# Two attention windows in sixteen steps: projections moved to even steps, short rounding and short rest moved ahead of the long ones

## Chip, cores and metric

The kernel runs on one core of a Trainium2 chip. The metric is device time in microseconds of one execution, lower is better. The engines are TensorE (PE, with its weight loads PEld), VectorE (DVE), ScalarE (ACT), GpSimd (POOL) and SyncE (SP), which here only issues transfers.

## What is computed

One transformer layer with latent attention and a gated feed-forward network side by side, on x of shape (2, 1024, 512) in float32:

```python
xn = layernorm(x)
q = rms_norm(xn @ wq_a.T, q_norm_w) @ wq_b.T      # 32 heads of 128 + 64
kv = xn @ wkv_a.T                                 # 64 latent + 64 rotary
k_nope, v = split(rms_norm(kv_c, kv_norm_w) @ wkv_b.T)
scores = (q_nope . k_nope + rope(q_pe) . rope(k_pe)) * scale   # causal
out = softmax(scores) @ v @ wo.T
return x + out + (silu(x1) * x2) @ w3.T + b3      # x1, x2 = xn @ w12.T + b12
```

## The kernel before

Three stages follow each other: `dense` (norm, latents, feed-forward), `attention`, and `combine` (output projection). The change is in `attention` alone.

Attention works on the latent keys: each head's query is projected straight into the latent space. The 32 windows are the 16 pairs of heads, each for the two batches (window w: heads of pair w // 2, batch w % 2). A window has 8 steps (u = s % 8), four for each of its two heads. A step takes two query tiles of 128 rows: the long tile of 8, 7, 6 or 5 blocks of 128 keys, and the short one of 1, 2, 3 or 4, so that every step has nine blocks in all. There are 256 steps in one stream, and each engine runs its own loop over them, held together by semaphores.

The path of a step s:

- TensorE: `scores` (L640) of the long and then of the short tile into `score_long` (two buffers) and `score_short` (one buffer; it waits for the short exponential of step s - 1). Then `transposes(s - 1)` (L657, matmuls L664) turns the short probabilities of the step before into `flip`, which has one buffer: it waits for `ptl_ready`, that is for `low_short(s - 2)`. Then `values(s - 5)` (L667). Then, in some steps, `project(n)` (L628), one of four pieces of a window's queries (n = 4 x window + piece), and once a window the block under `absorb_at` (L725): `absorb` (L609, only in every second window, for the weights of the next pair of heads) and `output_weights` (L620). Projection, absorption and output weights all write the one PSUM bank `proj`.
- VectorE: `least` (L852), the row minimum of the long and the short scores; in every second step `outputs`; then `low_long(s - 1)` (L857) and `low_short(s - 1)` (L863), what the rounding to 16 bits left over. `weights_low` (L869) does that for new weights, once per two windows.
- ScalarE: `exp` (L735) of the long and the short scores, `high_short(s - 1)` (L749) and `high_long(s)` (L742), the rounding to 16 bits, then `take(n)` (L761) of a projection, `query_high` (L756) for rotated queries, the copies after an absorption (`weights_latent`, L768, and `wo_out`, L805) and `weights_high` (L771).
- GpSimd, per half of a window's queries: four transfers that swap the halves of the rotary part (L822), `query_low` of the half before (L829, after `query_high`), two kinds of multiplies (L840, L842) and an addition (L846).
- SP: `turn(s)` (L568), the transposing transfer of the long probabilities' two 16-bit parts, used by `values(s)` five steps on (`LAG` = 5), the loads of new weights (`load_w`, `load_wo`) and the store of outputs.

`PIECE` (L524) says which projection runs in which step of a window: {step: (windows ahead, piece)}. `HIGH` says where `query_high` runs. `PIECE_FIRST` and `HIGH_FIRST` do it for the first window. A `take` waits until `query_low` of the piece four before it is done (L795), since they share a buffer.

Of the kernel before, what the change touches and what calls it, by code (L numbers as in the profile page):

```python
# [24 lines left out]
PAIRS = NH // 2  # L25
# [423 lines left out]
def attention(nc, io, scr, res):  # L449
# [9 lines left out]
    WINS = B * PAIRS  # L459
    WIN = ST  # L460
# [5 lines left out]
    with ExitStack() as ctx:  # L466
# [54 lines left out]
            return (tile(s, kind) + 1) * P  # L521


        PIECE = {0: (1, 3), 3: (2, 0), 4: (2, 1), 7: (2, 2)}  # L524
        PIECE_FIRST = {0: (1, 2), 1: (1, 3), 4: (2, 0), 5: (2, 1), 7: (2, 2)}
        HIGH = {1: (0,), 2: (1,), 5: (2,), 6: (3,)}
        HIGH_FIRST = {3: (0, 1), 6: (2, 3)}
        absorb_at, high_weights_at = lambda s: s % WIN == (2 if s < WIN else 1), lambda s: s % WIN == (3 if s < WIN else 2)

        def piece_at(s):  # L530

# [15 lines left out]
        @block.sync  # L547
        def _(sp):
            def load_w(p):
                j = p % 2  # L550
                sp.dma_start(raw[j][:].rearrange("p h c -> p (h c)"), io["wqk"][:, p, :]).then_inc(w_in[j], 16)
                sp.dma_start(wf[j][:, :, KVL:KVL + 2 * ROPE], io["wqp"][:, p, :, :]).then_inc(w_in[j], 16)

            def load_wo(pair):
                heads = slice(2 * pair, 2 * pair + 2)
                sp.dma_start(wv[:], io["wv"][:, heads, :]).then_inc(wo_in, 16)
                sp.dma_start(wo[:], io["wo"][:, heads, :]).then_inc(wo_in, 16)

            def swap_halves(k):

                c = k % 2
                sp.wait_ge(proj_out, 2 * k + 2)
                half = ROPE // 2
                for h, base in ((0, KVL), (1, 0)):
                    for to, of in ((base, base + half), (base + half, base)):
                        sp.dma_start(rot[to:to + half, c, :], qf[of:of + half, c, h, :]).then_inc(first_in[c], 16)

            def turn(s):  # L568

                sp.wait_ge(lo_ready, s + 1)  # L570
                if s >= NPT:
                    sp.wait_ge(pv_mm, s - NPT + 1)
                n = 2 * width(s, LONG)
                sp.dma_start_transpose(prob_t[:, s % NPT, 0:n // P, :], prob_hl[:, s % NHL, 0:n]).then_inc(turn_in[s % NPT], 16)

            def store(w):
                sp.wait_ge(o_ready, BLK * (w + 1))
                sp.dma_start(scr["o"][w // 2, w % 2], o[:, w % 2].rearrange("p t c -> p (t c)")).then_inc(o_out[w % 2], 16)

            load_w(0)  # L580
            load_w(1)
            for j, (dst, src) in enumerate(((ident, "ident"), (mask, "mask"))):
                sp.dma_start(dst[:], io[src]).then_inc(o_out[j], 16)
            for dst, src in ((sinT, "sinT"), (cosT, "cosT"), (kvw2, "kvw2")):
                sp.dma_start(dst[:], io[src]).then_inc(const_in, 16)
            load_wo(0)
            for k in range(2):
                swap_halves(k)
            sp.wait_ge(wl_ready, 1)
            load_w(2)  # L590
            for s in range(STEPS):
                w, u = s // WIN, s % WIN
                turn(s)
                if u == 2 and w % 2 == 1 and w + 1 < WINS:
                    sp.wait_ge(vo_mm, w + 1)
                    load_wo((w + 1) // 2)
                p = new_pair(w)
                if u == 3 and p is not None and p + 2 < PAIRS:
                    sp.wait_ge(wl_ready, p + 1)
                    load_w(p + 2)  # L600
                if u == LAG and w >= 1:
                    store(w - 1)
            store(WINS - 1)
            for j in range(2):
                sp.wait_ge(o_out[j], 16 * (WINS // 2 + 1))

        @block.tensor
        def _(pe):
# [88 lines left out]
            for s in range(STEPS + LAG):  # L697
                w, u = s // WIN, s % WIN
                if s < STEPS:
                    if u == 0 and w >= 1:  # L700
                        pe.wait_ge(ql_ready, 4 * w)
                    if s >= 2:
                        pe.wait_ge(exp_ready[LONG], s - 1)
                    scores(s, LONG)
                    if s >= 1:
                        pe.wait_ge(exp_ready[SHORT], s)
                    scores(s, SHORT)
                if s == 1:
                    pe.wait_ge(proj_out, 6)
                if 1 <= s <= STEPS:  # L710
                    transposes(s - 1)
                t = s - LAG
                if t >= 0:
                    if t % 2 == 0 and t >= 2:
                        pe.wait_ge(o_ready, t // 2)
                    values(t)
                if s < STEPS:
                    n = piece_at(s)
                    if n is not None:
                        pe.wait_ge(proj_out, n)  # L720
                        if n % 4 == 0:
                            pe.wait_ge(wl_ready, n // 8 + 1)
                            pe.wait_ge(wo_ready, w + 1)
                        project(n)
                    if absorb_at(s):  # L725
                        pe.wait_ge(proj_out, min(4 * (w + 2), 4 * WINS))
                        if w >= WINS - 2:
                            pe.wait_ge(wo_ready, w)
                        if new_pair(w) is not None:
                            absorb(new_pair(w))  # L730
                        output_weights(w)

        @block.scalar
        def _(act):
            def exp(s, kind):  # L735
                act.wait_ge(shift_ready[kind], s + 1)
                if s >= 2:
                    act.wait_ge(lo_ready if kind == LONG else flip_mm, s - 1)
                nc.scalar.activation(prob[kind][:, s % 2, 0:width(s, kind)], score_of(s, kind), ACT.Exp,  # L739
                                     bias=shift[:, s % (2 * WIN), kind:kind + 1], scale=-1.0).then_inc(exp_ready[kind], 1)  # L740
# [8 lines left out]
            def high_short(s):  # L749
                if s >= NPS:  # L750
                    act.wait_ge(pv_mm, s - NPS + 1)
                act.wait_ge(flip_mm, s + 1)
                n = width(s, SHORT)
                nc.scalar.activation(pth[:, s % NPS, 0:n], flip[:, 0:n], ACT.Copy).then_inc(pth_ready, 1)  # L754
# [29 lines left out]
            act.wait_ge(const_in, 16 * NCONST)  # L784
            for s in range(STEPS):
                w, u = s // WIN, s % WIN
                exp(s, LONG)
                exp(s, SHORT)
                if s >= 1:
                    high_short(s - 1)  # L790
                high_long(s)
                n = piece_at(s)
                if n is not None:
                    if n >= 8:
                        act.wait_ge(ql_ready, n - 7)  # L795
                    else:
                        act.wait_ge(first_low, n - 3)
                    take(n)
                for n in high_at(s):
                    query_high(n, rot_add, n - 3)  # L800
                if absorb_at(s):
                    act.wait_ge(vo_mm, w + 1)
                    if new_pair(w) is not None:
                        weights_latent(new_pair(w))
                    nc.scalar.activation(wo_out[:, w // 2, w % 2 * H // 2:(w % 2 + 1) * H // 2], of_out, ACT.Copy,  # L805
                                         scale=kvw2[:, 0:1]).then_inc(wo_ready, 1)
                if high_weights_at(s) and new_pair(w) is not None:
                    weights_high(new_pair(w))
# [42 lines left out]
        def _(dve):  # L851
# [5 lines left out]
            def low_long(s):  # L857
                dve.wait_ge(hi_ready, s + 1)
                n = width(s, LONG)
                nc.vector.tensor_tensor(prob_hl[:, s % NHL, n:2 * n], prob[LONG][:, s % 2, 0:n], prob_hl[:, s % NHL, 0:n],  # L860
                                        ALU.subtract).then_inc(lo_ready, 1)
# [55 lines left out]
            for s in range(STEPS + LAG):  # L917
                w, u = s // WIN, s % WIN
                if s < STEPS:
                    least(s, LONG)  # L920
                    least(s, SHORT)
                t = s - LAG
                if t >= 0 and t % 2 == 1:
                    outputs(t)
                if 1 <= s <= STEPS:
                    low_long(s - 1)
                    low_short(s - 1)
                if s < STEPS and high_weights_at(s) and new_pair(w) is not None:
                    weights_low(new_pair(w))


# [218 lines left out]
```

## Time and profile before

| what | value |
|---|---|
| time, median of 3 runs | 1473.96 us (1468.43 to 1487.34) |
| time of the profiled execution | 1476.83 us |
| its span, first to last instruction | 1475.1 us |
| TensorE busy over the span | 1297.4 us (88%) |
| VectorE busy | 1066.0 us (72%) |
| ScalarE busy | 939.9 us (64%) |
| GpSimd busy | 777.7 us (53%) |
| mean granted TensorE clock | 0.974 of full speed |

The span is that of one profiled execution, the median that of separate runs; the profiled execution is 2.87 us above the median. Busy time is a union over an engine's instructions, and the ends of matmuls are modelled, so a TensorE that shows as busy is not always at its peak. For lengths of TensorE work the distance from start to start is the safer reading.

### The profile page before, as it was taken

The numbers are of one execution on the slowest core, as the hardware profiler recorded it, in microseconds if no ns is written. First come the engines' busy times: TensorE is split into PE (matmuls) and PEld (weight loads), VectorE is DVE, ScalarE is ACT, GpSimd is POOL, SyncE is SP. The second block draws the span as 40 slices with busy tenths as digits, with TensorE's granted clock in tenths as the row PEclk, the third lists the DMA queues.
The fourth block names the chain that finished last, engine by engine and source line by source line (L and its number), as shares of the span: only waits on it lengthen the run. The fifth ranks groups of instructions, "written<-read, shape, count | busy, mean of one in ns | idle before, by whom it ended". The sixth has DMA issues, their size and how long they took to land. (4 is left out here: it accounts for less than half of the span.)

```text
span 1475.1 us, 32508 instructions
## 1 busy us (share of the span) xinstructions
PE 1297.4 (88%) x12930; PEld 887.4 (60%) x12930; DVE 1066.0 (72%) x1648; ACT 939.9 (64%) x1658; POOL 777.7 (53%) x759
## 2 busy tenths in 40 slices
PE   3899995899999999999988999999999998479988
PEld 3787773566666666666656666666666666234433
DVE  3755553788888889888888888888888889522321
ACT  3644541777777787787876778787787787612110
POOL 0222020877777777777766777777777872000100
PEclk9999996999999999999999999999999999799999
DMA  4011104698989989798897989889788897899995
GB/s 162 30 57 37 50 8 143 117 169 143 169 161 168 161 149 173 142 169 173 154 158 132 165 145 180 166 148 170 142 156 154 162 166 144 192 188 239 245 219 122
DMA packets 566982, 218.48 MB, mean 148 GB/s; under 512 B 508720, under 2 KB 548272, under 8 KB 566192
## 3 DMA queue, kind: packets, MB, share of 16 engines
q1 hardware_dynamic: 556336, 191.75, 69.0%
q0 software_dynamic: 10496, 24.66, 7.2%
q8 instruction: 103, 1.69, 0.5%
q14 instruction: 47, 0.39, 0.1%
HBM read 48.57 MB, written 25.17 MB: 50 GB/s over the span
## 5 line engine op out<-in xcount | busy, mean ns | idle before, releaser
L739 ACT ACTIVATE prob_long_sb<-score_long,shift_sb 128x1024 f32<-128x1024 f32 (+3 forms) x256 | 244.9, 957 | 219.3 <-DVE shift_sb L854 219.1
L860 DVE TENSOR_TENSOR prob_hl_sb<-prob_long_sb,prob_hl_sb 128x1024 f16<-128x1024 f32 (+3 forms) x256 | 335.7, 1311 | 0.0
L854 DVE TENSOR_REDUCE shift_sb<-score_long 128x1 f32<-128x1024 f32 (+3 forms) x256 | 260.0, 1016 | 71.6 <-PE score_long L654 67.8
L829 POOL TENSOR_TENSOR ql_sb<-qf_sb,qh_sb 128x512 f16<-128x512 f32 x124 | 145.0, 1170 | 204.2 <-ACT qh_sb L759 204.1
L747 ACT ACTIVATE prob_hl_sb<-prob_long_sb 128x1024 f16<-128x1024 f32 (+3 forms) x256 | 233.0, 910 | 0.0
L846 POOL TENSOR_TENSOR qf_sb<-qf_sb,rot_sb 64x512 f32<-64x512 f32 x124 | 183.7, 1482 | 9.5
L651 PE MATMUL score_long<-key_hi,qh_sb 128*128 128x512 f16 (+3 forms) x512 | 175.9, 344 | 9.5 <-DVE ql_sb L914 8.6
L685 PE MATMUL acc<-ch,prob_t_sb 128*128 128x65 f16 x1664 | 178.0, 193 | 0.0
L683 PE MATMUL acc<-ch,prob_t_sb 128*128 128x65 f16 x1664 | 177.6, 194 | 0.3 <-DMA prob_t_sb<-prob_hl_sb 0.3
L684 PE MATMUL acc<-cl,prob_t_sb 128*128 128x64 f16 x1664 | 177.7, 191 | 0.0
L664 PE MATMUL flip<-ident_sb,prob_short_sb 128*128 128x128 f32 x640 | 117.0, 281 | 65.4 <-DVE ptl_short_sb L866 65.3
L652 PE MATMUL score_long<-key_lo,qh_sb 128*128 128x512 f16 (+3 forms) x512 | 174.1, 340 | 0.0
L822 POOL DMA_DIRECT2D rot_sb<-qf_sb x248 | 124.3, 507 | 88.3 <-DVE ql_sb L914 62.1
L653 PE MATMUL score_long<-key_hi,ql_sb 128*128 128x512 f16 (+3 forms) x512 | 170.8, 340 | 0.0
L842 POOL TENSOR_TENSOR qf_sb<-qf_sb,cosT_sb 128x512 f32<-128x512 f32 x124 | 166.7, 1364 | 0.0
L685 PEld LDWEIGHTS acc<-ch,prob_t_sb 128*128 128x128 f16 x1664 | 153.3, 97 | 0.0
L684 PEld LDWEIGHTS acc<-cl,prob_t_sb 128*128 128x128 f16 x1664 | 152.9, 99 | 0.0
L683 PEld LDWEIGHTS acc<-ch,prob_t_sb 128*128 128x128 f16 x1664 | 152.4, 97 | 0.4 <-DMA prob_t_sb<-prob_hl_sb 0.4
L866 DVE TENSOR_TENSOR ptl_short_sb<-flip,pth_short_sb 128x128 f16<-128x128 f32 (+3 forms) x256 | 124.3, 485 | 22.6 <-ACT pth_short_sb L754 13.8
L739 ACT ACTIVATE prob_short_sb<-score_short,shift_sb 128x128 f32<-128x128 f32 (+3 forms) x256 | 134.2, 524 | 0.0
L664 PEld LDWEIGHTS flip<-ident_sb,prob_short_sb 128*128 128x128 f32 x640 | 68.6, 141 | 102.6 <-issue 96.7
L854 DVE TENSOR_REDUCE shift_sb<-score_short 128x1 f32<-128x128 f32 (+3 forms) x256 | 122.4, 478 | 0.2 <-PE score_short L654 0.2
(180 smaller groups left out, 3315.3 us busy)
## 6 DMA issues: line engine op xcount, KB each, us to landing
o<-o_sb SPq DMA_DIRECT2D x32, 512.0 KB, 4.1
o_nat_sb<-o SPq DMA_DIRECT2D x32, 512.0 KB, 6.7
rot_sb<-qf_sb POOLq DMA_DIRECT2D x248, 64.0 KB, 2.8
wo_sb<-wo SPq DMA_DIRECT2D x16, 512.0 KB, 4.2
wqk_sb<-wqk SPq DMA_DIRECT2D x16, 320.0 KB, 4.5
x_sb<-x SPq DMA_DIRECT2D x4, 1024.0 KB, 4.7
y<-y_sb SPq DMA_DIRECT2D x16, 256.0 KB, 2.0
prob_t_sb<-prob_hl_sb SPq DMA_TRANSPOSE x256, 4.7
```

What stands on the lines that cost most here:

```text
L651: nc.tensor.matmul(out, qh[:, row, q], key_hi[:, head, at], start=True, stop=False)
L652: nc.tensor.matmul(out, qh[:, row, q], key_lo[:, head, at], start=False, stop=False)
L653: nc.tensor.matmul(out, ql[:, row, q], key_hi[:, head, at], start=False, stop=not last)
L664: mm = nc.tensor.transpose(flip[:, at], prob[SHORT][:, s % 2, at], ident[:])
L683: nc.tensor.matmul(acc[:, at:at + KVL + 1], hi, high, start=(j == 0), stop=False)
L684: nc.tensor.matmul(acc[:, at:at + KVL], hi, low, start=False, stop=False)
L685: mm = nc.tensor.matmul(acc[:, at:at + KVL + 1], lo, high, start=False, stop=(j == i))
L739: nc.scalar.activation(prob[kind][:, s % 2, 0:width(s, kind)], score_of(s, kind), ACT.Exp, bias=shift[:, s % (2 * WIN), kind:kind + 1], sc ...
L747: nc.scalar.activation(prob_hl[:, s % NHL, 0:n], prob[LONG][:, s % 2, 0:n], ACT.Copy).then_inc(hi_ready, 1)
L846: nc.gpsimd.tensor_tensor(qf[rows, c, h, :], qf[rows, c, h, :], rot[rows, c, :], ALU.add).then_inc(rot_add, 1)
L854: nc.vector.tensor_reduce(shift[:, s % (2 * WIN), kind:kind + 1], score_of(s, kind), AX.X, ALU.min).then_inc(shift_ready[kind], 1)
L860: nc.vector.tensor_tensor(prob_hl[:, s % NHL, n:2 * n], prob[LONG][:, s % 2, 0:n], prob_hl[:, s % NHL, 0:n], ALU.subtract).then_inc(lo_rea ...
```

## The change

The projections of a window move from steps 0, 3, 4, 7 to 0, 2, 4, 6. The block under `absorb_at` moves from step 1 to step 3 and `weights_high` from step 2 to step 5 (all windows but the first), with the waits and loads that belong to them. On ScalarE `high_short(s - 1)` goes ahead of both exponentials, on VectorE `low_short(s - 1)` ahead of `low_long(s - 1)`, and `weights_low` runs one step after the `weights_high` it belongs to. No instruction of an engine is added or taken away.

```diff
-        PIECE = {0: (1, 3), 3: (2, 0), 4: (2, 1), 7: (2, 2)}
+        PIECE = {0: (1, 3), 2: (2, 0), 4: (2, 1), 6: (2, 2)}
...
-        absorb_at, high_weights_at = lambda s: s % WIN == (2 if s < WIN else 1), lambda s: s % WIN == (3 if s < WIN else 2)
+        absorb_at, high_weights_at = lambda s: s % WIN == (2 if s < WIN else 3), lambda s: s % WIN == (3 if s < WIN else 5)
...
-                if u == 2 and w % 2 == 1 and w + 1 < WINS:
+                if u == 4 and w % 2 == 1 and w + 1 < WINS:
                     sp.wait_ge(vo_mm, w + 1)
                     load_wo((w + 1) // 2)
                 p = new_pair(w)
-                if u == 3 and p is not None and p + 2 < PAIRS:
+                if u == (7 if w else 3) and p is not None and p + 2 < PAIRS:
                     sp.wait_ge(wl_ready, p + 1)
                     load_w(p + 2)
...
                         if n % 4 == 0:
                             pe.wait_ge(wl_ready, n // 8 + 1)
+                        if n % 4 == (0 if w == 0 else 1):
                             pe.wait_ge(wo_ready, w + 1)
                         project(n)
                     if absorb_at(s):
-                        pe.wait_ge(proj_out, min(4 * (w + 2), 4 * WINS))
+                        pe.wait_ge(proj_out, min(4 * (w + 2) + (1 if w else 0), 4 * WINS))
...
+                if s >= 1:
+                    high_short(s - 1)
                 exp(s, LONG)
                 exp(s, SHORT)
-                if s >= 1:
-                    high_short(s - 1)
                 high_long(s)
...
                 if 1 <= s <= STEPS:
+                    low_short(s - 1)
                     low_long(s - 1)
-                    low_short(s - 1)
-                if s < STEPS and high_weights_at(s) and new_pair(w) is not None:
+                if s < STEPS and s > 0 and high_weights_at(s - 1) and new_pair(w) is not None:
                     weights_low(new_pair(w))
```

## Rows read from the trace of the kernel before

**Rows 1.** Stretches: start:end, length, busy us (instructions) by engine, granted clock, DMA share, GB/s.
```profile
500.00:700.00 200.00, 185.10 (x2270) 129.53 (x2271) 174.99 (x260) 155.86 (x268) 148.85 (x141) 1.00 0.91 165
```

**Rows 2.** Line 805's own answer, 600 to 700 us: duration, first and last start.
```profile
L805 ACT ACTIVATE wo_out<-proj,kvw_sb x3: 481/493/494, 611.3 to 673.9; 128x256 f32<-128x256 f32 x3
```

**Rows 3.** Waits of the whole run: who waited for whom, us, times, longest.
```profile
ACT prob_long_sb L739 <- DVE shift_sb L854: 219.1, 206, 4.3
POOL ql_sb L829 <- ACT qh_sb L759: 204.1, 119, 4.2
...
PE flip L664 <- DVE ptl_short_sb L866: 65.3, 127, 2.6
...
PE score_short L651 <- ACT prob_short_sb L739: 13.0, 62, 0.7
```

**Rows 4.** Timeline of TensorE: start us, us, line, what, idle time before it.
```profile
601.23 0.39 PE L651 MATMUL score_long<-key_hi,qh_sb 128*128 128x512 f16 x1
...
602.82 0.61 PE L664 MATMUL flip<-ident_sb,prob_short_sb 128*128 128x128 f32 x4
603.26 0.19 PE L683 MATMUL acc<-ch,pth_short_sb 128*128 128x65 f16 x1
...
604.07 0.47 PE L637 MATMUL proj<-lat_hi,wq_h_sb 128*128 128x512 f32 x1
...
605.33 0.39 PE L651 MATMUL score_long<-key_hi,qh_sb 128*128 128x512 f16 x1
...
608.31 1.08 PE L616 MATMUL proj<-wqk_sb 128*128 128x64 f32 x8
609.32 0.65 PE L624 MATMUL proj<-wo_sb,wv_sb 128*64 128x256 f32 x4
...
620.61 0.63 PE L664 MATMUL flip<-ident_sb,prob_short_sb 128*128 128x128 f32 x4 [1.20 <-DVE ptl_short_sb L866]
```

**Rows 5.** Timeline of VectorE.
```profile
615.59 1.23 DVE L871 TENSOR_TENSOR wq_l_sb<-wq_f_sb,wq_h_sb 128x512 fp32r<-128x512 f32 x1 [0.88 <-ACT wq_h_sb L773]
...
618.08 1.92 DVE L860 TENSOR_TENSOR prob_hl_sb<-prob_long_sb,prob_hl_sb 128x768 f16<-128x768 f32 x1
619.92 0.55 DVE L866 TENSOR_TENSOR ptl_short_sb<-flip,pth_short_sb 128x384 f16<-128x384 f32 x1
...
625.03 1.07 DVE L854 TENSOR_REDUCE shift_sb<-score_long 128x1 f32<-128x896 f32 x1
```

**Rows 6.** Timeline of GpSimd.
```profile
617.92 3.21 POOL L842 TENSOR_TENSOR qf_sb<-qf_sb,cosT_sb 128x512 f32<-128x512 f32 x2
```

**Rows 7.** Groups by line and shape, 340 to 1280 us: count, busy us, mean ns, idle before.
```profile
L846 POOL TENSOR_TENSOR qf_sb<-qf_sb,rot_sb 64x512 f32<-64x512 f32 x114 | 168.2, 1476 | 8.8
...
L842 POOL TENSOR_TENSOR qf_sb<-qf_sb,cosT_sb 128x512 f32<-128x512 f32 x112 | 150.5, 1363 | 0.0
...
L829 POOL TENSOR_TENSOR ql_sb<-qf_sb,qh_sb 128x512 f16<-128x512 f32 x114 | 132.3, 1161 | 188.9 <-ACT qh_sb L759 188.9
...
L822 POOL DMA_DIRECT2D rot_sb<-qf_sb x224 | 112.2, 506 | 24.8 <-ACT qf_sb L764 20.1 <-issue 4.4
...
L840 POOL TENSOR_TENSOR rot_sb<-rot_sb,sinT_sb 128x512 f32<-128x512 f32 x56 | 105.3, 1880 | 5.0 <-DMA rot_sb<-qf_sb 4.9
...
L860 DVE TENSOR_TENSOR prob_hl_sb<-prob_long_sb,prob_hl_sb 128x640 f16<-128x640 f32 x60 | 88.7, 1479 | 0.0
...
L860 DVE TENSOR_TENSOR prob_hl_sb<-prob_long_sb,prob_hl_sb 128x1024 f16<-128x1024 f32 x59 | 71.9, 1218 | 0.0
```

**Rows 8.** Timeline of ScalarE.
```profile
627.04 0.47 ACT L739 ACTIVATE prob_short_sb<-score_short,shift_sb 128x256 f32<-128x256 f32 x1
...
628.40 0.64 ACT L759 ACTIVATE qh_sb<-qf_sb 128x512 f16<-128x512 f32 x1
```

**Rows 9.** The page's costliest groups: the long values, idle time before them and its cause.
```profile
L683 PE MATMUL acc<-ch,prob_t_sb 128*128 128x65 f16 x1664 | 177.6, 194 | 0.3 <-DMA prob_t_sb<-prob_hl_sb 0.3
```

**Rows 10.** DMA issues of the page: count, KB each, median us to landing.
```profile
wo_sb<-wo SPq DMA_DIRECT2D x16, 512.0 KB, 4.2
```

## The prediction

> **What bounds the kernel now.** I began with the stretches, to see which engine is nearest to full in the stage that the change touches. In a stretch of 200 us of the attention stage [rows 1] TensorE is busy 185.10 us (92.5%) at a granted clock of 1.00, VectorE 174.99 (87%), ScalarE 155.86, GpSimd 148.85. So TensorE leads, VectorE is close behind, and even a perfect order has only some 8% to give.
>
> Next the length of the repeating unit. The copy of L805 runs once per window; from its first to its third start [rows 2] two windows took 673.9 - 611.3 = 62.6 us. Two windows are the unit, since one absorption serves both. I call this a pair; 15 of them (windows 1 to 30) make up nearly the whole stage.
>
> Then the timeline of TensorE, for what a pair must cost if nothing waits [rows 4]. Starts are used, not durations, since matmuls overlap: scores of a step 602.82 - 601.23 = 1.59; four flips 603.26 - 602.82 = 0.44, so 0.11 a block; values 604.07 - 603.26 = 0.81; a projection 605.33 - 604.07 = 1.26; an absorption 609.32 - 608.31 = 1.01; output weights some 0.6. A pair has 16 steps, 40 flipped blocks, 8 projections, one absorption and two output weights: 16 x 2.40 + 40 x 0.11 + 8 x 1.26 + 1.0 + 1.2 = 55.1 us. So 62.6 - 55.1 = 7.5 us of a pair are stalls, with their restarts.
>
> The waits say which [rows 3]: 65.3 us of TensorE before the flips of L664, for ptl_short (L866), in 127 of 256 steps, and 13.0 before the short scores, for prob_short. The reader sees the first happen at 620.61: 1.20 us idle [rows 4], ended by the low_short that VectorE ran from 619.92 to 620.47 [rows 5]. In front of that low_short stood a low_long of 1.92 us. That is the pattern that the change goes at.
>
> **The change part by part.**
>
> *low_short ahead of low_long.* The next flip waits for low_short alone, so each ptl_short comes earlier by one low_long: 1.218 us in the mean for 1024 wide, 1.479 for 640 wide [rows 7]. That is as much as the longest stall I saw on it (1.20 us). low_long comes later by one low_short (0.55 us [rows 5], less for narrower ones). Behind it are the transposing DMA and the long values, four steps on; those waited 0.3 us in the whole run [rows 9], so this costs nothing. Were that cover gone, 0.55 us a step would be 9 us a pair.
>
> *high_short ahead of both exponentials.* Without this, low_short would still wait for ScalarE to finish two exponentials. ScalarE stands idle 219.1 us before the long exponential, waiting for its minimum [rows 3], about 0.9 us a step; a high_short copies at most 512 columns, no more than a query_high, which takes 0.64 [rows 8]. It now waits for the flips of its step, and the exponentials, high_long, the takes and the roundings of queries are queued behind it. In step 5 the flip ends 0.38 + 0.11 after the long scores and one block is rounded, while the minimum takes 1.07 [rows 5]: the minimum still comes last. In steps 3 and 7 (four short blocks 0.7, three flips 0.33, up to 0.64 for the rounding, a minimum of five blocks, well under 1.07) the rounding comes last, by some 0.8 us. Behind them stand step 3's absorption or output weights and the eight long blocks (1.36) of steps 4 and 0, which come before the next short scores. So I take nothing; the bounds are 0 and 0.8 us for each of four steps a pair.
>
> *Projections in steps 0, 2, 4, 6; absorption in step 3.* No matmul is added or removed. Before, steps 3 and 4, and 7 and 0, carried 1.26 us extra each while 5 and 6 carried none. Now every light step stands beside a heavy one.
>
> What is late next is the short score. Take step 5, which has no projection before or after the change. From the start of its minimum (625.03 [rows 5]) to the end of its short exponential (627.04 + 0.47 = 627.51 [rows 8]) is 2.48 us; 0.2 us lie ahead of it after the long scores, 0.06 behind (estimates from the same timelines). So 2.74 us pass between the long scores of step 5 and the short scores of step 6. TensorE meanwhile has two short blocks (0.38), one flip (0.11), values (0.81) and six long blocks (1.04): 2.34. That leaves a stall of 0.4, with a restart of 0.1 (620.47 to 620.61 is 0.14) 0.5 us. Steps 1 to 2 do the same now that the absorption has left step 1. Four per pair: 2.0 us.
>
> *weights_low one step behind weights_high.* Now VectorE waits 0.88 us for wh and then works 1.23 us [rows 5] just ahead of step 3's minimum, once per pair. After, weights_high runs at step 5 and weights_low at the end of step 6, without the wait. The 1.23 us stay, and I let 0.9 us of them (between 0 and 1.23) reach the next short score, since step 7 is light.
>
> *The waits moved on TensorE.* wo_ready now stands ahead of the projection of step 4, the wait on proj_out ahead of the absorption of step 3. Behind each are all later matmuls. The take of step 2 ends about 1.5 us before the absorption wants it, the copy of L805 about as long before step 4's projection, by laying the row durations end to end. Nothing, unless ScalarE is late (rival 3).
>
> *The loads on SP.* load_wo goes past two more turns, load_w past four; their waits are then long met. The loads land in 4.2 us [rows 10] beside the turns, which have the slack of [rows 9]. Nothing.
>
> *GpSimd.* GpSimd and VectorE get in each other's way: low_long is slower narrow than wide [rows 7], and two multiplies of L842, 1.363 us each by the mean, took 3.21 us together [rows 6] while the 1.92 us low_long ran [rows 5]. Because take(2,0) and take(2,2) now come ahead of the second query_high, the rotation starts 0.6 us later in the step, and shorter windows push it later still, onto low_longs of steps 1 and 5 that were clean. Each hit costs VectorE the rest of one GpSimd operation, between 0 and 1.4 us; the heavy step that follows absorbs most of it. I take 0.9 us a pair, between nothing and 4 x 1.4, nearer to nothing because of that room. On this the Trainium skill, "GPSIMD Engine Reference", section "Key points", says that GpSimd contends with VectorE instructions that have two SBUF inputs; that is low_long, and not low_short, whose first input is in PSUM. By that rule alone, with every low_long of steps 1 and 5 hit, the sum would be rival 2's; by the row means unchanged, it would be 0.9 us a pair lower than mine.
>
> **Sum.** 55.1 + 2.0 + 0.9 + 0.9 = 58.9 us a pair, 3.7 less than now. Times 15: 55.5. From the profiled execution's 1476.8: 1421 us. (That execution is 2.9 us above the median of the runs, 1473.96.)
>
> **Rivals.**
>
> 1. *The reorder reaches TensorE's floor.* If short scores hardly wait, a pair is 55.1 + 0.9 + 0.9 = 56.9: 5.7 x 15 = 86, so 1391. For it: VectorE's 54.8 (174.99/200 of a pair) is below the floor. Against: the chain of 2.74 us is there already.
>
> 2. *Contention eats half.* Four low_longs per pair meet half a GpSimd operation each, 4 x 0.73 = 2.9 us, and all of it reaches the minimum and so the short score. That is 2.0 more than my 0.9, a pair of 60.9: 1.7 x 15 = 25, so 1451. For it: [rows 6, 7]. Against: steps 2 and 6 have a projection, 1.26 us, behind the short score.
>
> 3. *Slower: a loop through GpSimd.* Before, the second query_high did not stand behind a take that waits for query_low of the first. Now take(2,0) in step 2 and take(2,2) in step 6 do. That closes a loop per half window: query_low 1.16, L840 1.88, L842 2 x 1.36, L846 2 x 1.48, four issues 4 x 0.51, query_low 1.16 [rows 7], a take and a query_high at some 0.64 each [rows 8]: 13.2 us. It decides from 15.65, half a window of now, that is when low_longs hold up GpSimd by 2.5 us more per half. With 16.2 a pair is 64.9: 2.3 x 15 = 35 more, 1511. For it: low_longs slide onto the chain. Against: query_low waits 204.1 us for ScalarE [rows 3], so the chain has room today.
>
> 4. *No gain.* Each stall on ptl_short turns into one on the short score (13.0 us now [rows 3]), because VectorE's minimum is what is late in both. A pair is 62.2, 1471. For it: VectorE runs without a gap through 618.08 to 620.47. Against: half of that was low_long, which no flip waits for any more.
>
> **How the numbers follow.** Chances: forecast 0.58 (pairs of 57.6 to 59.9: 1402 to 1436), rival 1 0.08, rival 2 0.17, rival 3 0.08, rival 4 0.09. Two per cent, about what a measurement of this kernel can tell from no change, is 29.5 us, some 2.0 us a pair. The forecast, rival 1 and the better third of rival 2 (0.06) are faster: 0.72. The rest of rival 2 and rival 4: 0.20 within. Rival 3: 0.08 slower. The range from 1388 to 1455 holds the forecast, rival 1 and most of rival 2, some 0.82.
>
> **What would show it.** Right: the wait of L664 on ptl_short falls from 65.3 to under 15 us; the short score's wait rises to 25 to 50; the copy of L805 repeats every 58 to 60 us per pair; TensorE is busy over 95%; VectorE's wait for wq_h is gone. Wrong: takes that wait for ql (rival 3), low_long means at 1.7 us and over (rival 2), or waits of L651 on prob_short beyond 70 us (rival 4). The forecast falls above all if ScalarE, now tied to the flips at the head of each step, starts its long exponential later than the minimum allows.

## The result, and the profile after

The changed kernel takes 1427.97 us (median of 3 runs, 1426.66 to 1437.23) against 1473.96 us before: a ratio of 0.9677 with a 95% interval of 0.9577 to 0.9776, faster by 3.2%. The profiled execution took 1437.23 us with a span of 1435.5 us, 40 us less than before's 1475.1. All of it lies in the attention stage. From the first scores of step 0 to those of step 255 it takes 951.2 us instead of 997.6 us; what lies ahead and behind, untouched by the change, went from 477.5 to 484.2 us, and is between 469.6 and 484.2 us in the profiled executions of this document. The profiled execution of the changed kernel is also the slowest of its three runs.

The stretch that answers to [rows 1], with the same columns:

```profile
500.00:700.00 200.00, 190.98 (x2373) 137.15 (x2373) 174.86 (x274) 167.27 (x285) 154.40 (x147) 0.99 0.98 174
```

TensorE went from 185.10 to 190.98 us of 200, 3.2% more, at a granted clock of 0.99 instead of 1.00, and 2373 matmuls stand in that time instead of 2270, 4.5% more. (The stretch begins at another place of a pair in the two traces, so the two shares can't be set against each other closely.) The transfer engines' share is 0.98, not 0.91. The two stretches behind it are less full:

```profile
700.00:900.00 200.00, 187.96 (x2351) 135.04 (x2348) 177.40 (x274) 166.47 (x282) 158.42 (x150) 1.00 0.93 168
900.00:1100.00 200.00, 189.99 (x2368) 136.55 (x2367) 177.55 (x272) 166.12 (x285) 153.46 (x147) 0.99 0.92 163
```

The copy that runs once per window, as in [rows 2], but from its first to its 31st start:

```profile
L806 ACT ACTIVATE wo_out<-proj,kvw_sb x31: 469/483/487, 308.5 to 1198.9; 128x256 f32<-128x256 f32 x31
```

That is (1198.9 - 308.5) / 15 = 59.4 us a pair, where 62.6 stood and 58.9 was forecast. Taken from the first scores of window 1 to those of window 31, as in all that follows, a pair was 62.72 before and is 59.47 now. The gain of 3.25 times 15 is 49 us; the first window gives 3.4 of it back (37.3 us instead of 33.9).

The waits of the changed kernel, those that answer to [rows 3] and the new ones (who waited for whom: us, times, longest):

```profile
POOL ql_sb L830 <- ACT qh_sb L760: 149.7, 79, 4.3
...
ACT pth_short_sb L755 <- PE flip L664: 115.7, 157, 3.0
...
POOL rot_sb L841 <- DMA rot_sb<-qf_sb: 39.7, 22, 3.9
...
ACT prob_long_sb L740 <- DVE shift_sb L855: 31.2, 80, 1.1
...
PE score_long L651 <- POOL ql_sb L830: 26.5, 27, 2.7
PE score_short L651 <- ACT prob_short_sb L740: 24.8, 67, 1.1
...
ACT qf_sb L765 <- POOL ql_sb L830: 9.4, 6, 1.6
...
DVE wq_l_sb L872 <- ACT wq_h_sb L774: 0.4, 1, 0.4
```

The line's own answer for the flips lists all that ended TensorE's idle time before them, and it is one line:

```profile
  ACT prob_short_sb L740: 2.6, 2
```

So the 65.3 us before the flips are gone. ScalarE's 219.1 us before the long exponential became 31.2, and 115.7 us now stand one instruction earlier, before high_short. The short scores wait 24.8 us instead of 13.0. And there is a wait that the prediction did not have: 26.5 us before the first long scores of a window, for GpSimd's query_low. GpSimd itself has less room: its wait for query_high fell from 204.1 to 149.7 us, and 39.7 us now go to waiting for the rotary swaps.

### The profile page after: what moved, and what is told of

It is laid out like the page before. It is cut to its first block and busy times, and to the rows that moved or that the text cites. A ratio compares the mean times of both kernels' runs of the same rounds, so it can differ in the third digit from the quotient of the medians.

```text
span 1435.5 us, 32537 instructions
## 1 busy us (share of the span) xinstructions
PE 1280.1 (89%) x12930; PEld 891.0 (62%) x12930; DVE 1033.0 (72%) x1648; ACT 950.3 (66%) x1658; POOL 772.0 (54%) x759
## 5 line engine op out<-in xcount | busy, mean ns | idle before, releaser
L861 DVE TENSOR_TENSOR prob_hl_sb<-prob_long_sb,prob_hl_sb 128x1024 f16<-128x1024 f32 (+3 forms) x256 | 319.3, 1247 | 0.0
L740 ACT ACTIVATE prob_long_sb<-score_long,shift_sb 128x1024 f32<-128x1024 f32 (+3 forms) x256 | 244.6, 955 | 31.4 <-DVE shift_sb L855 31.2
L830 POOL TENSOR_TENSOR ql_sb<-qf_sb,qh_sb 128x512 f16<-128x512 f32 x124 | 145.6, 1175 | 150.4 <-ACT qh_sb L760 149.7
L651 PE MATMUL score_long<-key_hi,qh_sb 128*128 128x512 f16 (+3 forms) x512 | 177.5, 347 | 36.1 <-POOL ql_sb L830 26.5
L847 POOL TENSOR_TENSOR qf_sb<-qf_sb,rot_sb 64x512 f32<-64x512 f32 x124 | 188.8, 1522 | 9.5
L755 ACT ACTIVATE pth_short_sb<-flip 128x128 f16<-128x128 f32 (+3 forms) x256 | 111.7, 436 | 116.6 <-PE flip L664 115.7
L843 POOL TENSOR_TENSOR qf_sb<-qf_sb,cosT_sb 128x512 f32<-128x512 f32 x124 | 172.8, 1414 | 0.0
L651 PEld LDWEIGHTS score_long<-key_hi,qh_sb 128*128 128x128 f16 x512 | 50.0, 98 | 116.7 <-issue 33.6
```

The lines of the kernel that those rows point to most:

```text
L651: nc.tensor.matmul(out, qh[:, row, q], key_hi[:, head, at], start=True, stop=False)
L843: op = nc.gpsimd.tensor_tensor(qf[:, c, h, :], qf[:, c, h, :], cosT[:, h, at], ALU.mult)
L847: nc.gpsimd.tensor_tensor(qf[rows, c, h, :], qf[rows, c, h, :], rot[rows, c, :], ALU.add).then_inc(rot_add, 1)
```

## The experiments

Ten kernels. Each ratio is to the kernel before, run beside it. A pair is from the trace as above: 15th part of the time from the first scores of window 1 to those of window 31. Before 62.72, changed kernel 59.47. Each pair is from one trace. The edit in the first window alone touches no other window, and yet its trace has 58.94: differences of half a microsecond between two traces say little.

| kernel | median us | ratio, 95% interval | pair us |
|---|---|---|---|
| both reorders, old places | 1415.98 | 0.9623 (0.9553 to 0.9693) | 59.05 |
| new places, old orders | 1437.33 | 0.9746 (0.9686 to 0.9805) | 59.68 |
| changed, ScalarE's order back | 1589.13 | 1.0789 (1.0727 to 1.0851) | 69.33 |
| changed, VectorE's order back | 1433.81 | 0.9709 (0.9653 to 0.9765) | 59.42 |
| before, ScalarE's reorder alone | 1469.87 | 0.9978 (0.9950 to 1.0006) | 62.30 |
| changed, load_w after the swaps | 1416.80 | 0.9602 (0.9561 to 0.9644) | 58.24 |
| changed, query_high ahead of take | 1406.15 | 0.9511 (0.9459 to 0.9562) | 58.49 |
| changed, weights_low at once in window 0 | 1419.12 | 0.9629 (0.9579 to 0.9679) | 58.94 |
| the last three together | 1397.33 | 0.9468 (0.9425 to 0.9512) | 57.43 |
| those, absorption back in step 1 | 1386.11 | 0.9431 (0.9375 to 0.9486) | 56.91 |

### Both reorders, old places

Edit, on the kernel before:

```diff
+                if s >= 1:
+                    high_short(s - 1)
                 exp(s, LONG)
                 exp(s, SHORT)
-                if s >= 1:
-                    high_short(s - 1)
                 high_long(s)
...
-                    low_long(s - 1)
                     low_short(s - 1)
+                    low_long(s - 1)
```

> The kernel before with the two reorders alone (short rounding first on ScalarE, short rest first on VectorE); projections, absorption and loads where they were. Theory (the reorders take away the stalls before the flips, the new places balance the steps): the wait of the flips on ptl_short falls from 65.3 to under 20 us, the time to 1440 to 1455. Rival (the places do nearly all, the reorders only change which wait ends last): 1465 to 1480, with the short score's wait on prob_short up from 13 to over 40 us.

Measured: 1415.98 us, 24 us below what the theory gave. The reorders alone do as much as the whole change or more; the intervals overlap. Idle time before the flips, from that line's answer, and two waits:

```profile
  ACT prob_short_sb L739: 2.6, 2
  issue: 0.3, 1
```

```profile
PE score_short L651 <- ACT prob_short_sb L739: 41.9, 96, 2.1
...
PE score_long L651 <- POOL ql_sb L829: 0.8, 2, 0.5
```

The flips no longer wait for ptl_short, as the theory said. What the rival said of the next wait holds too: the short scores' wait rose to 41.9 us. The time is far from the rival's.

### New places, old orders

Edit, on the changed kernel: both orders as before.

> The changed kernel with both orders put back; only the new steps of projections, absorption, weight rounding and loads are left. Theory: flips still wait for ptl_short, over 40 us, and the time is 1445 to 1465. Rival (places do nearly all): 1425 to 1435.

Measured: 1437.33 us, 2.3 us above the rival's range and below the theory's. Its interval against the kernel before, 0.9686 to 0.9805, is clear of no change, but not of a change of two per cent. From its waits:

```profile
PE score_long L651 <- POOL ql_sb L830: 21.5, 31, 2.4
...
PE score_short L651 <- ACT prob_short_sb L740: 11.0, 58, 0.2
...
PE flip L664 <- DVE ptl_short_sb L867: 8.3, 13, 1.8
```

The flips' wait fell to 8.3 us with both orders as before. That is a miss of mine: I expected over 40. The new places alone take most of those stalls away; they are projections, absorption, weight rounding and loads together, and which of these does it was not separated. So before the flips the two halves of the change do the same job. In time they do not add up either: from 62.72 us a pair, the orders alone reach 59.05, the places alone 59.68, both together 59.47. The waits show one reason. The places bring TensorE a wait on query_low, 21.5 us here and 26.5 in the changed kernel, that the old places don't have (0.8 us). Beside the reorders they lower the short score's wait, from 41.9 to 24.8 us. What the places give is hidden by what they cost: once three repairs below have taken that wait down to 3.6 us, a pair is 57.43, 1.62 below the orders alone. The repairs were not run on the old places, so how much of this belongs to the places is not shown.

### Changed kernel, ScalarE's order back

```diff
-                if s >= 1:
-                    high_short(s - 1)
                 exp(s, LONG)
                 exp(s, SHORT)
+                if s >= 1:
+                    high_short(s - 1)
                 high_long(s)
```

> The changed kernel with ScalarE's order put back (both exponentials ahead of the short rounding), VectorE's short rest still first. Theory: the short rest now waits for ScalarE, with low_long queued behind it, so VectorE idles and the time rises by 10 to 30 us over the changed kernel (1438 to 1458). Rival (the rounding at the head only delays exponentials): 1420 to 1430.

Measured: 1589.13 us, over 150 us slower than the changed kernel, five times the top of what I gave it. Its waits, then a step on VectorE and on ScalarE:

```profile
ACT prob_long_sb L740 <- DVE shift_sb L855: 321.9, 254, 2.8
...
DVE ptl_short_sb L867 <- ACT pth_short_sb L755: 278.8, 255, 1.8
```

```profile
705.74 0.82 DVE L855 TENSOR_REDUCE shift_sb<-score_long 128x1 f32<-128x640 f32 x1
...
708.37 0.56 DVE L867 TENSOR_TENSOR ptl_short_sb<-flip,pth_short_sb 128x384 f16<-128x384 f32 x1 [1.22 <-ACT pth_short_sb L755]
708.85 1.75 DVE L861 TENSOR_TENSOR prob_hl_sb<-prob_long_sb,prob_hl_sb 128x768 f16<-128x768 f32 x1
710.52 1.21 DVE L855 TENSOR_REDUCE shift_sb<-score_long 128x1 f32<-128x1024 f32 x1
```

```profile
706.59 0.79 ACT L740 ACTIVATE prob_long_sb<-score_long,shift_sb 128x640 f32<-128x640 f32 x1 [0.49 <-DVE shift_sb L855]
707.28 0.68 ACT L740 ACTIVATE prob_short_sb<-score_short,shift_sb 128x512 f32<-128x512 f32 x1
707.85 0.49 ACT L755 ACTIVATE pth_short_sb<-flip 128x384 f16<-128x384 f32 x1
```

Read across the two: minimum (705.74), long exponential (706.59), short exponential (707.28), rounding (707.85), then VectorE's short rest (708.37), its long rest (708.85) and the next minimum (710.52). Each of these waits for the one before it, on two engines by turns: 255 of 256 short rests wait for ScalarE. A step is that whole circle, 4.78 us here, 69.33 / 16 = 4.33 in the mean. With low_long in front of low_short, as before, VectorE has work for the time that ScalarE takes (in the changed kernel a low_long takes 1.1 to 1.6 us in the mean, by its width); with high_short in front of the exponentials, ScalarE has it done. In the new places, only the reorder on VectorE without that on ScalarE closes the circle.

### Changed kernel, VectorE's order back

```diff
-                    low_short(s - 1)
                     low_long(s - 1)
+                    low_short(s - 1)
```

> The changed kernel with VectorE's order put back (long rest ahead of short rest), ScalarE's short rounding still first. Theory: flips wait again behind low_long, over 25 us, 1435 to 1450. Rival (with balanced steps the flips do not wait for it any more): within 5 us of the changed kernel, 1423 to 1433.

Measured: 1433.81 us, and 59.42 us a pair against 59.47. The time lies between the two ranges, 0.8 us above the rival's; the pair and the flips' wait of 7.1 us, where the theory had over 25, are the rival's. In the new places, beside ScalarE's reorder, no worth of VectorE's order can be told. Its flips:

```profile
PE flip L664 <- DVE ptl_short_sb L867: 7.1, 15, 1.3
```

### Kernel before, ScalarE's reorder alone

Formed after these four: perhaps ScalarE's order alone does it. Edit: the first half of the first diff.

> The kernel before with ScalarE's short rounding moved ahead of the exponentials and nothing else; VectorE's order and all places as before. Theory formed after the first four runs (what ends the stalls before the flips is ScalarE's order: the short rounding fills ScalarE's idle time, so that rounding and rest of the long tile follow earlier; VectorE's order adds little): 1415 to 1430, flips' wait on ptl_short under 25 us. Rival (both reorders are needed in the old places, since low_short still stands behind low_long): 1445 to 1465, flips' wait over 35 us.

Measured: 1469.87 us, a ratio of 0.9978 (0.9950 to 1.0006): no difference that can be told. My second theory fell, and the rival's flips are what the trace has, though its time is not:

```profile
PE flip L664 <- DVE ptl_short_sb L866: 50.8, 122, 1.3
```

In the old places the flips do wait for a low_short that stands behind low_long, and VectorE's reorder on top of ScalarE's is worth 62.30 - 59.05 = 3.25 us a pair. So what VectorE's reorder is worth depends on ScalarE's and on the places: a gain of 3.25 us a pair in the old places beside ScalarE's, nothing in the new places beside it (59.42 to 59.47), and a loss of 9.65 in the new places without it (59.68 to 69.33). VectorE's reorder alone in the old places was not run.

### Changed kernel, load_w after the swaps

In the changed kernel, among windows 1 to 29, the even ones take 28.2 to 31.2 us and the odd ones, which have the absorption, 28.6 to 31.8. A long even one (window 6, 443.67 to 474.88), on SP, GpSimd and TensorE:

```profile
450.90 0.57 SPq L551 DMA_DIRECT2D wqk_sb<-wqk  x1
451.52 0.43 SPq L552 DMA_DIRECT2D wq_f_sb<-wqp  x1
```

```profile
451.14 2.01 POOL L823 DMA_DIRECT2D rot_sb<-qf_sb  x4
...
461.39 1.29 POOL L841 TENSOR_TENSOR rot_sb<-rot_sb,sinT_sb 128x512 f32<-128x512 f32 x1 [3.86 <-DMA rot_sb<-qf_sb]
```

```profile
474.88 0.39 PE L651 MATMUL score_long<-key_hi,qh_sb 128*128 128x512 f16 x1 [2.65 <-POOL ql_sb L830]
```

load_w was moved to step 7, but it stands behind that step's turn, and so goes out at 450.90, 7.2 us into the next window, at the moment when GpSimd issues its swaps (451.14). The last swap lands 8.2 us after the last issue; GpSimd idles 3.86 us, and 13.5 us later the next window's first scores wait 2.65 us for query_low. Window 26 (1042.59 to 1071.25), which has no load, for comparison:

```profile
1050.06 2.01 POOL L823 DMA_DIRECT2D rot_sb<-qf_sb  x4
...
1056.41 1.27 POOL L841 TENSOR_TENSOR rot_sb<-rot_sb,sinT_sb 128x512 f32<-128x512 f32 x1
```

Its swaps land 4.2 us after the last issue, and GpSimd goes on without idling. Not every load does this. Of the twelve even windows with one, six (4, 6, 8, 16, 20, 22) take 30.1 to 31.2 us, their swaps land 6.8 to 8.2 us after the last issue, and the waits on query_low at their ends, 1.95 to 2.66 us each, make up 14.2 of the 26.5 us. In the other six the load goes out earlier, 6.4 to 6.7 us into the window (6.7 to 7.5 in the long ones), the swaps land within 6.3 us, and the window takes 28.2 to 29.1.

The longest windows have no load. They are 5, 9 and 23, each right behind such a wait, with 31.8 us where the odd windows next to them take 29.7 to 29.9. Window 5, its head, and its first scores:

```profile
411.90:443.70 31.80, 30.18 (x357) 21.78 (x358) 26.86 (x42) 24.99 (x44) 22.97 (x23) 0.95 0.73 139
412.60:415.95 3.35, 3.35 (x28) 2.46 (x27) 1.43 (x3) 0.77 (x3) 3.35 (x3) 0.50 0.95 242
```

```profile
411.85 0.39 PE L651 MATMUL score_long<-key_hi,qh_sb 128*128 128x512 f16 x1 [2.32 <-POOL ql_sb L830]
```

TensorE had waited 2.32 us for query_low (1.95 and 2.32 ahead of windows 9 and 23) and had just begun again when its granted clock fell to 0.50, the lower of its two levels, 1.2 GHz. Behind the three other waits, of 2.65, 2.33 and 2.66 us ahead of windows 7, 17 and 21, it stayed at 1.00. (The trace of the kernel before has one such fall, in window 16, behind a wait of 2.59 us before the flips.) So a wait on query_low cost its own time and, three times, some 2.1 us more: 6.3 us in all, 0.42 of a pair. Edit:

```diff
-                if u == (7 if w else 3) and p is not None and p + 2 < PAIRS:
-                    sp.wait_ge(wl_ready, p + 1)
-                    load_w(p + 2)
+                if w % 2 == 0 and u == (2 if w else 3):
+                    p = new_pair(w - 1) if w else 1
+                    if p is not None and p + 2 < PAIRS:
+                        sp.wait_ge(wl_ready, p + 1)
+                        load_w(p + 2)
```

> The changed kernel with load_w moved three turns further, to step 2 of the window after, so that it is issued after the rotary swaps of step 1 have landed. Theory (the load that the change moved to step 7 is issued late, among the swaps of the next window's step 1; these land 5 to 8 us after their issue instead of 4, GpSimd starts its rotation late and the next window's first scores wait for its query_low): the swaps of step 1 land within 4.5 us in all windows, TensorE's wait on ql falls from 26.5 to about 12 us, time 10 to 20 us below the changed kernel (1408 to 1418). Rival (GpSimd's chain is simply full, the swaps' landing is a symptom): within 5 us of the changed kernel.

Measured: 1416.80 us and a pair of 58.24, 1.23 less than the changed kernel. In this trace the clock does not fall in windows 1 to 30, which is 0.42 of the 1.23. The ratio's interval, 0.9561 to 0.9644, overlaps the changed kernel's, 0.9577 to 0.9776, so the gain in time rests on the waits in the traces:

```profile
POOL rot_sb L843 <- DMA rot_sb<-qf_sb: 19.9, 16, 2.1
PE score_long L653 <- POOL ql_sb L832: 13.0, 22, 0.9
```

The waits are as the theory had them: TensorE's on query_low fell from 26.5 to 13.0 us, the longest from 2.7 to 0.9, and GpSimd's on the swaps from 39.7 to 19.9. The landing was not always within 4.5 us: the swaps of step 1 still took 5.2 to 6.4 us in ten windows of thirty, so the load was about half of the delay, not all.

### Changed kernel, query_high ahead of take

```diff
+                if s >= WIN:
+                    for n in high_at(s):
+                        query_high(n, rot_add, n - 3)
                 n = piece_at(s)
...
-                for n in high_at(s):
-                    query_high(n, rot_add, n - 3)
+                if s < WIN:
+                    for n in high_at(s):
+                        query_high(n, rot_add, n - 3)
```

> The changed kernel with ScalarE's query_high ahead of the take of the same step (all windows but the first). Theory (the earlier take stands in front of the second query_high, GpSimd's last query_low comes 0.6 us and more later, and the next window's first scores wait for it by 0.13 to 0.65 us even in windows without a late load): TensorE's wait on ql falls from 26.5 to about 8 us, time 10 to 15 us below the changed kernel. Rival (that wait only comes from late swaps): within 5 us of the changed kernel.

Measured: 1406.15 us, a pair of 58.49.

```profile
PE score_long L651 <- POOL ql_sb L834: 11.1, 23, 1.4
```

The theory's direction holds: 26.5 us became 11.1 (8 were expected), with load_w where the changed kernel has it, and although GpSimd waits longer for the swaps (67.7 us, where the changed kernel has 39.7). The pair's 0.98 times 15 is 14.7 us, in the range given; 0.42 of the 0.98 is the clock, which does not fall in windows 1 to 30 of this trace either. The median fell by more, 21.8 us, of which the trace does not account for 7.

### Changed kernel, weights_low at once in the first window

The projection of step 4 in window 0, and what VectorE did just before:

```profile
278.37 0.77 PE L637 MATMUL proj<-lat_hi,wq_h_sb 128*128 128x512 f32 x1 [5.05 <-issue]
```

```profile
276.53 1.75 DVE L872 TENSOR_TENSOR wq_l_sb<-wq_f_sb,wq_h_sb 128x512 fp32r<-128x512 f32 x1
```

The wait is put down to "issue", but weights_low ends at 278.28, and the projection, which waits for wl_ready, starts at 278.37.

```diff
-                if s < STEPS and s > 0 and high_weights_at(s - 1) and new_pair(w) is not None:
+                if (s < WIN and high_weights_at(s) or s >= WIN and s < STEPS and high_weights_at(s - 1)) and new_pair(w) is not None:
```

> The changed kernel with weights_low in the same step as weights_high in the first window only, as before. Theory (in the first window the projection of step 4 waits for it; 5.05 us idle there against 1.66 before): the first window falls from 37.3 to about 34 us, the time by 3 us. Rival: the stall comes from elsewhere, and nothing changes.

Measured: the first window takes 33.8 us instead of 37.3, as expected. The median, 1419.12 us, is 8.9 below the changed kernel's; the 3.5 us of the window are shown, the rest is within what these medians vary by.

### The three together

> The changed kernel with all three: load_w at step 2 of the window after, query_high ahead of take, weights_low at once in the first window. Theory: the gains add up but for an overlap in the wait on ql, 20 to 30 us below the changed kernel (1398 to 1408), pairs of windows near 57.5 us. Rival (short scores and GpSimd's contention set the pace): 1412 to 1425.

Measured: 1397.33 us, at the lower end of the theory, and a pair of 57.43. The interval, 0.9425 to 0.9512, lies wholly below the changed kernel's. The wait on query_low is nearly gone; that of the short scores remains:

```profile
PE score_long L653 <- POOL ql_sb L836: 3.6, 16, 0.5
...
PE score_short L653 <- ACT prob_short_sb L742: 24.1, 67, 1.3
```

### Those, with the absorption back in step 1

```diff
-        absorb_at, high_weights_at = lambda s: s % WIN == (2 if s < WIN else 3), lambda s: s % WIN == (3 if s < WIN else 5)
+        absorb_at, high_weights_at = lambda s: s % WIN == (2 if s < WIN else 1), lambda s: s % WIN == (3 if s < WIN else 5)
...
-                        if n % 4 == (0 if w == 0 else 1):
+                        if n % 4 == 0:
                             pe.wait_ge(wo_ready, w + 1)
...
-                        pe.wait_ge(proj_out, min(4 * (w + 2) + (1 if w else 0), 4 * WINS))
+                        pe.wait_ge(proj_out, min(4 * (w + 2), 4 * WINS))
```

> The version with the three repairs, its absorption and output weights put back from step 3 to step 1, a step without a projection. Theory (the short scores of step 2 wait because step 1 has too little TensorE work for the chain minimum, long exponential, short exponential, 2.7 us): the stall before the short scores of step 2 goes, that of step 6 stays, a pair of windows falls by 0.6 to 1.0 us from 57.4, the time by 9 to 15 us from that version's (about 1383 to 1390). Rival (the copy of the output weights then holds up the projection of step 2 or the exponentials behind it): no change or slower, 1395 to 1410.

Measured: 1386.11 us, a pair of 56.91.

```profile
PE score_short L653 <- ACT prob_short_sb L742: 18.3, 36, 1.7
```

Idle time before the short scores of step 2 (means over windows 2 to 29, even and odd) was 0.29 and 0.26 us with the absorption in step 3 and is gone; that of step 6 stays (0.36 and 0.49 us). The pair fell by 0.52, a little under the 0.6 expected and no more than traces differ by, and the time is inside its range. Its median is the lowest here, 0.9431 of the kernel before (0.9375 to 0.9486): faster than both kernels, but not to be told from the version with the three repairs, whose interval overlaps. That the stall goes is shown; what it is worth in time is not.

## Why the prediction was right, and where not

The time, 1427.97 us, lies 7 us above the 1421 forecast and inside the forecast case's own range; the pair, 59.47, is 0.57 above 58.9. By the steps of the prediction:

**TensorE's floor, 55.1 us a pair: no run contradicts it.** The best version came to 56.91.

**The flips' stalls go: right, but not for the reason given alone.** They went from 65.3 us to none. The prediction credited the reorders. They do it together, and so do the places without them (8.3 us left). And the two reorders were priced one by one, as if each stood for itself. They do not: ScalarE's alone is worth nothing in the old places, and VectorE's without ScalarE's costs 161 us in the new ones (1589 against 1428). The sentence "without this, low_short would still wait for ScalarE" named the link, but gave it no price; it was the largest price in the case.

**The short score's stall, 2.0 us a pair: right.** Idle time before the short scores is 0.24 and 0.43 us in steps 2 and 6 of even windows, 0.36 and 0.30 in odd ones (means over windows 2 to 29), 1.33 a pair; with four restarts of 0.1 that is 1.7. The wait in the whole run, 24.8 us, is just under the 25 to 50 named. The last experiment shows the cause: work in the light step removes it. In steps 0 and 4, behind those in which the rounding comes last, no short score waits: the nothing put down for ScalarE's reorder held.

**weights_low, 0.9 us a pair: too much.** No short score waits in step 7 of odd windows or in step 0 behind it, so no cost of it is seen there. In the first window, which the prediction left out, the same edit cost 3.4 us.

**GpSimd's contention, 0.9 us: the hits came, the cost was not seen.** The narrow and wide low_longs, as in [rows 7]:

```profile
L861 DVE TENSOR_TENSOR prob_hl_sb<-prob_long_sb,prob_hl_sb 128x1024 f16<-128x1024 f32 x59 | 91.8, 1556 | 0.0
...
L861 DVE TENSOR_TENSOR prob_hl_sb<-prob_long_sb,prob_hl_sb 128x640 f16<-128x640 f32 x60 | 66.2, 1103 | 0.0
```

The 1024 wide ones, those of steps 1 and 5, rose from 1.218 to 1.556 us, as said, 0.34 us each where rival 2 needed 0.73; four of them are 1.35 us a pair. But the 640 wide ones fell from 1.479 to 1.103, and all low_longs together from 311.3 to 295.7 us, about 1.0 a pair less. (low_short, which reads PSUM, shows no such spread: its 128x384 form took 0.54 to 0.56 us all 64 times in either trace.) The prediction counted only the rise. No run here prices contention in a pair; what the later GpSimd chain cost came out elsewhere.

**The loads on SP cost nothing: this step failed.** load_w was laid against the turns and their slack alone, not against the swaps on GpSimd's queue. Its wait is met, but it stands behind a turn, and goes out among the swaps of the next window. Moving it away halved TensorE's wait on query_low and took 1.23 us off a pair, 0.42 of it by the clock.

**Rival 3 was half of what happened.** Its loop (take behind query_low, second query_high behind take) was right in its links: takes now wait 9.4 us for query_low, and putting query_high first took 0.98 us off a pair, 0.42 of it by the clock. But it had no end on TensorE. The wait on ql_ready ahead of a window's first scores was in the code and was not in the sum; it measured 26.5 us, 1.8 a pair. With weights_low's 0.9 and contention's 0.9 not showing where they were put, the sum came out near by terms that cancel: that the time fell so close to 1421 is in part luck.

**What would show it.** The copy repeats every 59.4 us, inside 58 to 60; TensorE is busy 95.5% in the stretch of [rows 1], but 94.0 and 95.0% in the two behind it, so the sign of over 95% is met only there; VectorE's wait for wq_h fell from 13.9 to 0.4 us; low_long stayed under 1.7 in the mean. The takes' wait for query_low, rival 3's sign, is there with 9.4 us.

## What to carry to other kernels

When two engines hand work to each other in order, price a reorder on one together with that on the other: here the pair was worth 3.7 us of 62.7, one half alone was worth nothing, and the other half without its partner, tried in the new places, cost 9.65. When a transfer or a copy is moved, ask what it goes out beside, not only whether its own wait is met, and follow the engine that it delays to the next wait on the busiest engine. Two halves of a change can remove the same stalls, and one of them can bring a wait of its own that hides what else it gives; so don't expect the gains of both, and look for the new wait before you give one half up. When the busiest engine waits, look at its granted clock behind the wait too.

## What the runs showed of the hardware

In the changed kernel, four swaps of 64 KB each, SBUF to SBUF, issued in step 1, land 3.2 to 6.2 us after the last issue in windows with no load of weights (4.2 in window 26). With 448 KB of weights issued within a microsecond of the first of them they land up to 8.2 us after it (window 6). The transfer engines' share is 0.98 in window 26 and 1.06 in window 6.

TensorE's granted clock fell to 0.50, 1.2 GHz, at the head of windows 5, 9 and 23, just behind waits of 2.32, 1.95 and 2.32 us, and not behind waits of 2.65, 2.33 and 2.66; each fall made its window some 2.1 us longer.

Putting VectorE's short rest first while ScalarE's rounding stood behind its exponentials, in the new places, made a circle of 4.33 us a step of two engines that are busy 87% and 84% of a stretch in the changed kernel: 16.6% slower than that kernel by the pair.
